# Splitting a graph network's gate operands for fp32r, with the rests made early and the kept state on GpSimd

## What is computed

```python
m = gelu(h_E @ m0_w + m0_b); m = gelu(m @ m1_w + m1_b); m = gelu(m @ m2_w + m2_b)
dh = segment_sum(m, src, 512) / 30
h = layer_norm(x + dh, ln1_g, ln1_b)
d = gelu(h @ d0_w + d0_b); d = gelu(d @ d1_w + d1_b); d = d @ d2_w + d2_b
x = layernorm(x + layer_norm(h + d, ln2_g, ln2_b))
# second layer: attention among the 8 heads of each node, then messages over the edges
Q, K, V = x @ Wq, x @ Wk, x @ Wv                      # each (512, 8, 32)
x1 = softmax(Q K^T / sqrt(32)) V                      # 8 x 8 per node
h = layernorm(x + segment_sum(x1[dst] * x1[src], dst) @ O_w + O_b)
h = layernorm(h + relu(h @ f1_w + f1_b) @ f2_w + f2_b)
gi, gh = h @ gru_w_ih + b_ih, h @ gru_w_hh + b_hh     # each (512, 768): r, z, n
r, z = sigmoid(gi_r + gh_r), sigmoid(gi_z + gh_z)
n = tanh(gi_n + r * gh_n)
x = layernorm(x + (1 - z) * n + z * h)
```

## Time and profile before

| what | value |
|---|---|
| median of 3 runs | 595.21 us (594.47 to 595.46) |
| profiled execution, its own time | 594.7 us |
| its span | 592.6 us |
| PE busy | 573.7 us, 97% |
| DVE busy | 462.4 us, 78% |
| ACT busy | 369.1 us, 62% |
| POOL busy | 224.1 us, 38% |
| mean granted clock of PE | 0.999 |

### The profile page before, as it was taken

How to read it: one execution, slowest core, us unless ns; L and a number is a source line. 1 busy time by engine, 2 the same in 40 slices (tenths; PEclk the granted TensorE clock), 3 DMA queues, 4 the chain that set the end, 5 groups by cost and what they waited for, 6 DMA issues and landing times.

```text
span 592.6 us, 8599 instructions
## 1 busy us (share of the span) xinstructions
PE 573.7 (97%) x3032; PEld 487.7 (82%) x3032; DVE 462.4 (78%) x795; ACT 369.1 (62%) x565; POOL 224.1 (38%) x211
## 2 busy tenths in 40 slices
PE   7989999999999999999999999999999999898895
PEld 6778888888888888888888888888888889577763
DVE  5986497778878887788998789879766566798667
ACT  6866786777777766777766778757275543311242
POOL 4075577556666544554444555430000000000011
PEclk9999999999999999999999999999999999999999
DMA  8255487285576636546553875223182404000000
GB/s 295 79 205 175 143 288 218 106 285 172 170 223 189 215 106 214 160 155 212 178 192 128 319 239 164 91 81 91 46 317 74 152 0 143 0 2 0 1 0 35
DMA packets 34504, 86.86 MB, mean 147 GB/s; under 512 B 3872, under 2 KB 23200, under 8 KB 29856
## 3 DMA queue, kind: packets, MB, share of 16 engines
q1 hardware_dynamic: 27264, 67.09, 36.0%
q0 software_dynamic: 6912, 19.10, 8.5%
q10 hardware_dynamic: 288, 0.13, 0.1%
HBM read 66.69 MB, written 19.62 MB: 146 GB/s over the span
## 4 chain that ended last, share of the span: by engine, by line
PE 83%; DVE 10%; ACT 2%; issue 2%; POOL 1%; DMA 1%; POOLq 0%; DVEq 0%; ACTq 0%
PE ps L1337 27%; PE ps L1389 10%; PE ps L1543 7%; PE ps L1395 5%; PE ps L1371 5%; PE ps L1432 5%; PE ps L1367 4%; PE ps L1366 4%; PE ps L1507 4%; PE ps L1434 2%; PE ps L1585 2%; PE ps L1636 1%; PE ps L1555 1%; PE ps L1574 1%; PE ps L1351 1%
## 5 line engine op out<-in xcount | busy, mean ns | idle before, releaser
L483 POOL DMA_INDIRECT sorted_rows<-m,place x120 | 167.1, 1393 | 151.5 <-ACT m L546 123.5
L529 ACT ACTIVATE m_hi<-ps,cols 128x512 fp32r<-128x512 f32 x128 | 88.6, 692 | 67.0 <-PE ps L1337 41.5
L864 DVE TENSOR_TENSOR m_lo<-m_out,m_hi 128x512 fp32r<-128x512 f32 x128 | 88.5, 693 | 51.2 <-ACT m_out L531 48.2
L1337 PE MATMUL ps<-x_hi,w_hi 128*128 128x512 f32 x248 | 97.0, 391 | 0.5 <-DVE x_lo L738 0.5
L1337 PE MATMUL ps<-x_lo,w_hi 128*128 128x512 f32 x248 | 96.9, 391 | 0.0
L1337 PE MATMUL ps<-x_hi,w_lo 128*128 128x512 f32 x248 | 96.7, 390 | 0.0
L531 ACT ACTIVATE m_out<-ps,cols 128x512 f32<-128x512 f32 x128 | 88.5, 691 | 1.8 <-DVE m_lo L864 1.8
L738 DVE TENSOR_TENSOR x_lo<-x_raw,x_hi 128x1024 fp32r<-128x1024 f32 x62 | 73.1, 1218 | 5.3 <-ACT x_hi L523 5.3
L1389 PE MATMUL ps<-w_lo,m_hi 128*128 128x256 f32 x256 | 64.2, 283 | 0.0
L1389 PE MATMUL ps<-w_hi,m_hi 128*128 128x256 f32 x256 | 64.0, 282 | 0.0
L546 ACT ACTIVATE m<-m_in 128x512 f32<-128x512 f32 x64 | 39.5, 634 | 38.0 <-DVE m_in L877 38.0
(11 more groups left out here) (229 smaller groups left out, 1136.7 us busy)
## 6 DMA issues: line engine op xcount, KB each, us to landing
x_raw<-in_edges_dram SPq DMA_DIRECT2D x31, 1024.0 KB, 6.1
sorted_raw<-sorted_rows SPq DMA_DIRECT2D x24, 647.5 KB, 4.6
sorted_raw<-sorted_rows SPq DMA_DIRECT2D x6, 518.0 KB, 4.0
d_w<-in_d_dram SPq DMA_DIRECT2D x3, 1024.0 KB, 8.7
d_w<-in_d_dram SPq DMA_DIRECT2D x1, 3072.0 KB, 10.4
rows<-in_rows_dram SPq DMA_DIRECT2D x1, 2176.0 KB, 10.2
sorted_rows<-m,place POOLq DMA_INDIRECT x120, 4.8
w_raw<-in_w_dram SPq DMA_DIRECT2D x4, 256.0 KB, 5.4
```

Source lines behind the costliest of these rows:

```text
L483: pool.indirect_dma_start(out=sorted_d, out_offset=bass.IndirectOffsetOnAxis(ap=place[:, at:at + 1], axis=0), in_=m2[:, b % 2, t], in_offs ...
L529: nc.scalar.activation(out_hi[:, m], ps[:, bank], ACT.Gelu, bias=col(bias, m)).then_inc(hi_signal, 1)
L864: nc.vector.tensor_tensor(lo[:, m], m_out[:, m], hi[:, m].bitcast(F32), ALU.subtract).then_inc(done, 1)
L1337: last = nc.tensor.matmul(out, left, right, start=(k == 0 and i == 0), stop=(k == KE - 1 and i == 2))
```

## The change

It does the following. (1) The gates become fp32r products of three passes: two tiles of weights `gru_hi` and `gru_lo` (1024 columns: r, z and n of `w_ih`, then n of `w_hh`) lie over the first part of `d1_w`, and two tiles of activations `gate_hi` and `gate_lo` over `qk_rows`. ACT rounds the weights behind its bias copies, DVE subtracts before it makes the bias constants. ACT writes the turned rows twice, as `gate_hi` and as `act_T`; the rest of half 0 is made by DVE between the residual sums of chunks 2 and 3, that of half 1 by POOL. Both n parts of a chunk are one 512-column product. (2) The kept state goes from DVE to POOL, in front of each chunk's own power and behind that of the chunk before. (3) The score products of chunk 0 are made in two halves, with the wait for the power between them, and PE begins to add up at the first half. (4) The reduction of chunk 3's scores is moved up, and chunks 2 and 3 share one softmax. (5) PE gathers chunk 1 before it adds up the output products of chunk 2. The number of transfers doesn't change.

```diff
+        gru_mem = ExitStack()
+        mem[0] = gru_mem
+        gru_hi = sb("gru_hi", [P, KH, 4 * H], F32R)
+        gru_lo = sb("gru_lo", [P, KH, 4 * H], F32R)
+        gru_mem.close()
         mem[0] = ctx
         d1_w = sb("d1_w", [P, KD, D])
...
+        gate_hi = sb("gate_hi", [P, KH, N], F32R)
+        gate_lo = sb("gate_lo", [P, KH, N], F32R)
+        gate_act_mem.close()
...
+        def gate_rest(half):
+
+            part = (slice(None), slice(None), HALF[half])
+            return gate_lo[part], act_T[part], gate_hi[part].bitcast(F32), ALU.subtract
...
+            def keep_part(c):
+
+                pool.wait_ge(rz_sig, c + 1)
+                pool.wait_ge(gru_out_rows, c // 2 + 1)
+                pool.tensor_tensor(kept[:, c], h_rows[:, c], rz[:, c, H:2 * H], ALU.mult).then_inc(kept_product, 1)
+                pool.wait_ge(kept_product, c + 1)
+                pool.tensor_tensor(kept[:, c], kept[:, c], xp[:, c], ALU.add).then_inc(kept_ready, 1)
+
             for c in range(NC):
-                inverse_std([c])
+                if c:
+                    inverse_std([c - 1])
+                keep_part(c)
+                if c == 0:
+                    pool.wait_ge(gate_act, 8)
+                    pool.tensor_tensor(*gate_rest(1)).then_inc(gate_split, 1)
+            inverse_std([NC - 1])
...
+            act.wait_ge(d1w_split, KD)
+            act.wait_ge(rz_weights, 1)
+            for w_in, at in ((w_ih, 0), (w_hh, 3 * H)):
+                n = 3 * H if at == 0 else H
+                nc.scalar.activation(gru_hi[:, :, at:at + n], w_in[:, :, 3 * H - n:], ACT.Copy).then_inc(gru_hi_done, 1)
...
-            affine(0, "t_ln2_w", "t_ln2_b")
+            def gate_inputs(half):
+
+                turned[0] += 1
+                act.wait_ge(hat_turned, turned[0])
+                for out in (gate_hi, act_T):
+                    for k in range(KH):
+                        nc.scalar.activation(out[:, k, HALF[half]], turned_bank(half, k), ACT.Identity,
+                                             bias=col("t_ln2_b", k), scale=col("t_ln2_w", k)).then_inc(gate_act, 1)
+
+            gate_inputs(0)
...
                     written.append(step(nc.vector.tensor_tensor(res[:, c], product(c), add[:, c], ALU.add)))
+                    if behind_first and c == chunks[0]:
+                        behind_first()
...
+            dve.wait_ge(gru_hi_done, 2)
+            for w_in, at in ((w_ih, 0), (w_hh, 3 * H)):
+                n = 3 * H if at == 0 else H
+                nc.vector.tensor_tensor(gru_lo[:, :, at:at + n], w_in[:, :, 3 * H - n:], gru_hi[:, :, at:at + n].bitcast(F32),
+                                        ALU.subtract).then_inc(gru_split, 1)
             link(nc.vector.tensor_scalar(two_ones[0:33], ident[0:33], 0.0, None, ALU.mult))
...
             dve.wait_ge(d2_done, NC)
-            moments(NODE_HALF[1])
-            score_products(0).then_inc(prod_ready, 1)
+            variance(NODE_HALF[1])
+            score_products(0, slice(0, DH // 2))
+            dve.wait_ge(rstd_ready, norms[0])
             hats_written(1, lambda c: normed(res, xp, c))
-            score_products(1).then_inc(prod_ready, 1)
+            score_products(0, slice(DH // 2, DH))
+            score_products(1)
...
+            made = step(nc.vector.tensor_tensor(*last_scores()))
             scores(2, 4)
-            less_top(2)
-            softmax(2, 3)
+            dve.wait_ge(dve_step, made)
+            link(nc.vector.tensor_reduce(probs[:, 3], last_scores()[0], AX_X, ALU.add))
+            less_top(2, 4)
+            softmax(2, 4, 3)
             out_products(2).then_inc(prod_ready, 1)
-            link(nc.vector.tensor_reduce(probs[:, 3], view, AX_X, ALU.add))
-            less_top(3)
-            softmax(3, 4)
...
+            def rest_gate():
+
+                dve.wait_ge(gate_act, 4)
+                nc.vector.tensor_tensor(*gate_rest(0)).then_inc(gate_split, 1)
...
-                norm(half, f2_done, product_rows, skip)
-                rows_after(half, "t_ln2_w", "t_ln2_b", None, hats[0])
-            dve.wait_ge(skip_ready, skips[0])
+                norm(half, f2_done, product_rows, skip, rest_gate if half else None)
+                rows_after(half, "t_ln2_w", "t_ln2_b", None, hats[0], gru_out_rows)
...
                 link(nc.vector.tensor_tensor(res[:, c], one_less_z[:, c], cand[:, c], ALU.mult))
-                dve.wait_ge(dve_step, kept_at)
+                dve.wait_ge(kept_ready, c + 1)
                 link(nc.vector.tensor_tensor(res[:, c], res[:, c], kept[:, c], ALU.add))
...
                 for j in range(parts):
+                    if j * len(counts) % parts == 0:
+                        pe.wait_ge(ready, counts[j * len(counts) // parts])
...
             gather(0)
-            add_up(2, OUT_BANK[2])
-            for s in range(1, NC):
-                gather(s)
+            gather(1)
+            add_up(2, OUT_BANK[2], prod_ready, (6,))
+            gather(2)
+            gather(3)
...
-                for k in range(KH):
-                    last = nc.tensor.matmul(ps[:, bank], act_T[:, k, c * P:(c + 1) * P], w_ih[:, k, 0:2 * H], start=False,
-                                            stop=(k == KH - 1), skip_group_check=True)
...
+                pe.wait_ge(gate_act, 4 * (c // 2) + 2)
+                for i, at in enumerate((0, 2 * H)):
+                    n = slice(at, at + 2 * H)
+                    for a, w_part in ((gate_hi, gru_hi), (gate_hi, gru_lo), (gate_lo, gru_hi)):
+                        if i == 0 and a is gate_lo:
+                            pe.wait_ge(gate_split, c // 2 + 1)
+                        for k in range(KH):
+                            last = nc.tensor.matmul(ps[:, bank + i], a[:, k, e], w_part[:, k, n], start=False,
+                                                    stop=(k == KH - 1 and a is gate_lo), skip_group_check=True)
+                    last.then_inc(rz_done if i == 0 else gru_done, 1)
```

More of the change, by code:

```diff
@@ L281, in turned_bank, with last_scores, halves_of @@
             return ps[:, 2 + half, k * NH:(k + 1) * NH]
+        def gate_rest(half):
+            part = (slice(None), slice(None), HALF[half])
+            return gate_lo[part], act_T[part], gate_hi[part].bitcast(F32), ALU.subtract
+        def last_scores():
+            q = qk_rows[:, 3, 0:H].rearrange("p (h a d) -> p h a d", h=HEADS, a=1)
+            k = qk_rows[:, 3, H:2 * H].rearrange("p (a g d) -> p a g d", a=1, g=HEADS)
+            part = [P, HEADS, HEADS, DH]
+            out = prod[3].rearrange("p (h g d) -> p h g d", h=HEADS, g=HEADS)
+            return out, q.to_broadcast(part), k.to_broadcast(part), ALU.mult
+        def halves_of(c):
+            half = HEADS * H // 2
+            return prod[c][:, 0:half], prod[c][:, 0:half], prod[c][:, half:], ALU.add
         def row_half(r):
@@ L702, in _ @@
             affine(1, None, None)
-            exponential(0, 1)
-            exponential(1, 2)
+            exponential(0, 1, 1)
+            exponential(1, 2, 2)
             qkv(2)
@@ L1051, in normed, with sums_and_stats @@
                                                ALU.subtract, ALU.mult)
-            def sums_and_stats(chunks, done, product, add):
+            def sums_and_stats(chunks, done, product, add, behind_first=None):
                 written = []
@@ L1062, in sums_and_stats, with norm @@
                 link(ins)
-            def norm(half, done, product, add):
-                sums_and_stats(NODE_HALF[half], done, product, add)
+            def norm(half, done, product, add, behind_first=None):
+                sums_and_stats(NODE_HALF[half], done, product, add, behind_first)
                 moments(NODE_HALF[half])
@@ L1076, in hats_written, with rows_after @@
                 hats[0] += len(NODE_HALF[half])
-            def rows_after(half, weight, bias, add, hat_count):
+            def rows_after(half, weight, bias, add, hat_count, written=None):
                 dve.wait_ge(hat_ready, hat_count)
@@ L1083, in rows_after @@
                 link(nc.vector.tensor_tensor(out[:, cs], hat[:, cs], row_half(row(weight)), ALU.mult))
-                nc.vector.tensor_tensor(out[:, cs], out[:, cs], row_half(add if add else row(bias)), ALU.add).then_inc(skip_ready, 1)
-                skips[0] += 1
+                last = nc.vector.tensor_tensor(out[:, cs], out[:, cs], row_half(add if add else row(bias)), ALU.add)
+                if written:
+                    last.then_inc(written, 1)
+                else:
+                    last.then_inc(skip_ready, 1)
+                    skips[0] += 1
             skips = [0]
```

101 lines of the change are left out of this document (46 added, 55 removed).

## The result

The changed kernel takes 598.43 us (598.30 to 600.48, 6 runs), the kernel before 595.13 on the same chip: 3.3 us slower by the medians. The ratio, in which every run counts and not only the middle ones, is 1.007 [1.006, 1.008], or about 4.0 us (means of 598.99 and 595.00).

The account below looks back on a forecast made before the run. TensorE alone bounds up to 497.5 us, then the chain passes back and forth, starting with VectorE. 594.7 + 3.1 - 1.0 + 0.2 = 597.0, with 0.3 for the median 597.3 us; range 594.3 to 598.9.

Parts of the forecast that it names:

- the clock: Rival, 7%: TensorE stands still some 3 us before the projections, its clock falls to 1.2 GHz, about +2.5, 599.8 us.
- Part 1: Behind d1: ScalarE's two weight roundings and VectorE's two subtractions delay the second residual add, +3.1 us (0.9 to 3.4).
- Part 2: Attention: split score product, one softmax for two chunks, moved gather, with GpSimd's power held by the half product: -1.0 us.
- the last gather 2.1 later: Sign in attention that the forecast is right: TensorE's last gather starts 2.1 us later in the span, at 545.7.
- Part 3: Gates in the tail: TensorE's pace falls from 4.3 to 3.6 us a chunk, its last product ending 3 us sooner.
- Part 4: ScalarE, VectorE and GpSimd in the tail: kept state and exclusion give a pace of 3.75, +0.2 us (-1.5 at best).
- Then its second kept operation gets between the two steps of VectorE's last rows (574.1 becomes 574.7): Tail, half 1: GpSimd's kept operation delays VectorE's last rows from 574.1 to 574.7.
- the assumption that GpSimd holds VectorE: Tail: GpSimd, once reading SBUF, holds VectorE as long as it is held; without this the tail gives -0.9.
- over 4 us later: Argument against the clock's fall: after the last gate product the granted clock only fell over 4 us later.
- GpSimd holding nothing: Rival, 20%: GpSimd is held by VectorE but never holds it; the tail gives 0.9, time 596.2 us.
- the kept state free: Rival, 12%: in the tail GpSimd's kept state delays nothing, the pace is VectorE's 3.1, time 593.5 us.
- the rests covered: Rival, 8%: the weights' rests are covered or made elsewhere, Part 1 is 0 to 0.9, time 594.2 to 595.1.

Follow-up runs that it names:

- the 592.6: Changed kernel with rests made earlier, GpSimd's kept state placed by VectorE's PSUM reads, statistics or waits, and half 1's rest on VectorE: 592.60 us.
- the warm kernel: Changed kernel with 16 instead of 4 of TensorE's warming products between d2 and the turning of xp: 598.16 us, ratio 1.0052.
- the two series: The changed kernel's first six runs and its repetition without any further change, each beside the kernel before: 598.43 and 598.86 us.

## Why the prediction was off

The direction was right, and 598.43 lies within 594.3 to 598.9; the size was not: +2.1 was forecast, and the medians give +3.3, the ratio of all runs about +4.0. Two terms of the sum failed, the tail and the clock.

- **Part 1, the rests:** +3.1 forecast, +3.03 measured. Right, with its reason: from 497.50 the chain is VectorE's own. That TensorE stands still meanwhile is the clock's matter, below.
- **Part 2, attention:** -1.0 forecast, -1.11 measured, and the power at 1.59 beside the half product. Right. In the changed kernel the sign named for both Parts, the last gather 2.1 later, was missed: the gathers end at 549.79 where it was 545.64, which less the 0.65 of the start is 3.5, with the clock's share in it.
- **Part 3, TensorE's pace:** 3.6 as forecast (its biases of chunks 2 and 3 start at 580.85 and 584.46). What it is worth in the changed kernel no run shows; it is worth 1.8 us once VectorE needs 3.24 a chunk. The reading that the old pace of 4.1 was TensorE's own is half right: in the profile before chunks 0 to 2 are 3.96 and 3.94 apart, which is VectorE's 3.1 and the kept state's 0.85, and only the last, 4.30, has a wait for the gates.
- **Part 4, the tail:** +0.2 forecast, +1.02 measured. The failed step is "Then its second kept operation gets between the two steps of VectorE's last rows (574.1 becomes 574.7)". GpSimd's operations got among the two norms instead. I had taken a norm, with one tensor and two columns in SBUF, as free; it is held: 1.66 instead of 0.74. That makes the turned rows, ScalarE's four pieces and GpSimd's rest late too. The rest, put at 575.3 to 576.6, ran from 576.10 to 577.39 when the 4.10 us are taken off by which TensorE's gates were late: 0.8 later, which is the difference between +0.2 and +1.02. The pace behind it, 3.75, was right (3.8), and so was the assumption that GpSimd holds VectorE.
- **The clock:** zero forecast, 0.8 to 1.5 measured. The step that failed is the argument "over 4 us later" from the earlier trace rows. One reading of one execution was no bound: here the clock fell 2.2 us after the last warming product in one execution (504.76 to 507.0), and 4.6 us after it in another (504.19 to 508.75), when TensorE had already turned rows again.
- **The rivals:** GpSimd holding nothing, the kept state free, and the rests covered are all refuted by rows above. But the rests can be covered by placing alone, and so can the kept state once the gates are split: both together, with the attention parts, make the 592.6.

Even at the end of the program the moment of the fall varies. TensorE's last product ends at 582.65 both in the kernel with the kept state back on VectorE and in the one with the first kept state later. The windows in which the clock falls are, in this order:

```profile
584.50:585.00 0.50, 0.00 (x0) 0.00 (x0) 0.47 (x2) 0.00 (x0) 0.00 (x0) 0.64 0.28 96
```

```profile
587.50:588.00 0.50, 0.00 (x0) 0.00 (x0) 0.17 (x1) 0.00 (x0) 0.22 (x1) 0.64 0.56 205
```

A mean of 0.64 is a fall after 0.14 us of the window: 2.0 us after the last product in one, 5.0 in the other. So "over 4 us" was one value of several, and taking it for a bound was the error.

The sum of S1 and S2 is 3.03 - 1.11 + 1.02 = 2.94 without the clock, and the warm kernel has 2.9 by the same stretches and 3.0 by the median. With the short fall's 0.8 it is 3.7, where the medians of the two series show 3.3 and 3.9; with the long fall's 1.5 it is 4.5. Why one execution has the short and another the long fall stays open.

## What to carry to other kernels

Work put "under" a stage is hidden only on the engine that has a gap there; place it by that engine's own idle rows, here two blocks earlier, and count what falls idle behind a delay, because TensorE's clock can add to it (0.8 to 1.5 us here). GpSimd beside VectorE is cheap or dear by what VectorE does at that moment: put its operations beside statistics, waits and operations with an operand in PSUM, and keep them from norms and from sums and products with both inputs in SBUF. With the split gates, S2 is 22.05 with the kept state on VectorE, 22.49 with it on GpSimd as the change places it, and 19.97 placed (and the second rest on VectorE): unplaced it lost 0.4 us in four chunks, placed it won 2.1.

## What the runs showed of the hardware

A norm of 256 elements (one SBUF tensor, two SBUF columns as scalars) is held by a GpSimd operation that reads SBUF: 0.78 instead of 0.41, two of them 1.66 instead of 0.74; statistics (0.42 beside 0.74) aren't. The Trainium skill, "SBUF — State Buffer", section "Who interferes with whom", counts `tensor_scalar`, which a norm is, among the operations that can take both port pairs, and so contend. The prediction had taken over only the rule on two SBUF inputs; the trace agrees with both (the norm's 0.78, and the multiplication's 1.31). The granted clock went to 0.50 (1.2 GHz) around the same wait of 2.89 us at different moments, and stayed there for 3.4 to 6.8 us, though TensorE had work again for most of them.
